# Small blocks' third layer as three split products, its weights through the ring of four stages

## What is computed

```python
h = gelu(x @ w1[e] + b1[e])        # 512 -> 1024, exact gelu
h = gelu(h @ w2[e] + b2[e])        # 1024 -> 1024
expert_out = h @ w3[e] + b3[e]     # 1024 -> 512
out = sum over the 2 best experts of gate * expert_out
```

## Time and profile before

| | us |
|---|---|
| median of 3 runs | 1721.82 |
| lowest, highest | 1720.84, 1722.42 |
| the profiled execution, its time | 1722.78 |
| its span in the trace | 1720.9 |

### The profile page before, as it was taken

One profiled execution on the slowest core, in us unless ns is written; L12 is line 12 of the kernel. 1 busy time (PEld: TensorE's weight loads), 2 busy tenths in 40 slices (PEclk: granted clock), 3 DMA queues, 4 the chain that ended last, 5 costly groups with the idle time before them and its releaser, 6 DMA issues.

```text
span 1720.9 us, 40335 instructions
## 1 busy us (share of the span) xinstructions
PE 1704.8 (99%) x15462; PEld 1509.2 (88%) x15462; DVE 1209.4 (70%) x2807; ACT 931.6 (54%) x1652; POOL 180.1 (10%) x271
## 2 busy tenths in 40 slices
PE   9999999999999999999999999999999999999997
PEld 8888888898889888988898878777899999999997
DVE  5677777777777777777775575566677777777773
ACT  4655656565556555655555454455545555545551
POOL 2010110111011101110110100000011010110100
PEclk9999999999999999999999999999999999999999
DMA  9982322222222222221215499998666666667662
GB/s 296 371 316 77 83 89 78 66 83 88 67 77 83 88 68 77 83 89 46 80 33 182 174 367 384 348 353 285 200 214 214 212 205 206 209 224 226 219 197 49
DMA packets 128181, 292.72 MB, mean 170 GB/s; under 512 B 19610, under 2 KB 42842, under 8 KB 128040
## 3 DMA queue, kind: packets, MB, share of 16 engines
q1 hardware_dynamic: 104616, 225.46, 38.8%
q0 software_dynamic: 23424, 65.30, 12.8%
HBM read 244.04 MB, written 46.66 MB: 169 GB/s over the span
## 4 chain that ended last, share of the span: by engine, by line
PE 88%; DVE 2%; issue 1%; ACT 1%; DMA 0%; POOLq 0%; POOL 0%; DVEq 0%; ACTq 0%
PE bank_rows L2301 21%; PE bank_rows L750 13%; PE bank_rows L736 12%; PE bank_rows L2316 7%; PE bank_rows L803 6%; PE bank_rows L2355 5%; PE bank_rows L791 4%; PE bank_rows L814 3%; PE bank_rows L2341 3%; PE bank_rows L2382 3%; PE bank_rows L830 2%; PE bank_rows L773 2%; PE bank_rows L894 2%; DVE probs L1470 1%; PE bank_rows L2393 1%
## 5 line engine op out<-in xcount | busy, mean ns | idle before, releaser
L1145 ACT ACTIVATE probs<-probs,neg_max 100x726 f32<-100x726 f32 x256 | 228.9, 896 | 168.1 <-DVE neg_max L1470 168.1
L2545 DVE TENSOR_TENSOR w_low<-stage,w_high 128x1024 fp32r<-128x1024 f32 x176 | 213.3, 1223 | 35.5 <-ACT w_high L2449 35.0
L1470 DVE CUSTOM_DVE_ANT_0 probs<-bank_rows,mask_sb 100x726 f32<-100x726 f32 x256 | 222.9, 909 | 16.4 <-PE bank_rows L791 14.8
L2449 ACT ACTIVATE w_high<-stage 128x1024 fp32r<-128x1024 f32 x176 | 183.9, 1057 | 33.4 <-DMA stage<-in_L_ffn_w 33.2
L2472 ACT ACTIVATE gelu<-bank_rows,biases 128x256 f32<-128x256 f32 x176 | 82.3, 474 | 216.4 <-PE bank_rows L2301 211.7
L1151 ACT ACTIVATE p_t<-bank_rows 122x1200 f32<-122x1200 f32 x128 | 146.4, 1168 | 95.8 <-PE bank_rows L803 95.8
L2301 PE MATMUL bank_rows<-h_high,w_high 128*128 128x256 f32 x704 | 196.5, 279 | 0.0
L2301 PE MATMUL bank_rows<-h_low,w_high 128*128 128x256 f32 x704 | 196.5, 279 | 0.0
L2301 PE MATMUL bank_rows<-h_high,w_low 128*128 128x256 f32 x704 | 196.5, 279 | 0.0
L736 PE MATMUL bank_rows<-ctx_high,wk_high 128*128 128x360 f32 (+1 forms) x512 | 175.7, 343 | 3.3 <-DVE v_even L1451 2.1
L736 PE MATMUL bank_rows<-ctx_low,wk_high 128*128 128x360 f32 (+1 forms) x512 | 167.8, 328 | 0.0
(11 more groups left out here) (245 smaller groups left out, 3869.9 us busy)
## 6 DMA issues: line engine op xcount, KB each, us to landing
stage<-in_L_ffn_w SPq DMA_DIRECT2D x240, 512.0 KB, 4.7
plain_w<-in_L_ffn_w SPq DMA_DIRECT2D x15, 2048.0 KB, 12.4
expert_in_rows<-filling POOLq DMA_DIRECT2D x8, 3341.0 KB, 25.2
router_rows<-in_gate_rows POOLq DMA_DIRECT2D x112, 200.0 KB, 3.4
ctx_raw<-in_ctx SPq DMA_DIRECT2D x16, 720.0 KB, 4.9
ctx_raw<-in_ctx SPq DMA_DIRECT2D x15, 724.0 KB, 4.3
xs_sb<-expert_in_rows SPq DMA_DIRECT2D x11, 514.0 KB, 5.4
b_sb<-in_L_ffn_b SPq DMA_DIRECT2D x19, 256.0 KB, 4.9
```

Of the source, the lines that this page charges most:

```text
L1145: nc.scalar.activation(p, p, ACT.Exp, bias=neg_max[:, h:h + 1], scale=-1.0, accum_out=exp_sum[:, h:h + 1]).then_inc(probs_ready, 1)
L1470: nc.vector.tensor_tensor_reduce(out=pieces(probs[:, q, :]), in0=slots_of(q)[0:S, :, 0:PIECE], in1=pieces(mask_sb[:]), scale=-1.0, scalar= ...
L2449: nc.scalar.activation(hi, src, ACT.Copy).then_inc(chunk_hi[which], 1)
L2545: nc.vector.tensor_tensor(lo, src, hi.bitcast(F32), ALU.subtract).then_inc(chunk_lo[which], 1)
```

## The change

w3 of the small blocks is no longer loaded plain. SP loads it in four pieces of two rows of tiles (load_third), through the same ring of stages, each after DVE has subtracted piece 4 + i of the same block's w2. ACT makes the high part (third_high), DVE the low one (third_low), into the buffers that the big blocks use for w3. The first four pieces of the next block's w2 wait for third_low where they waited for the subtractions of w2's pieces 4 to 7. The AHEAD pieces wait for third_low(7). The second gelu is done twice for each tile (once to fp32r, once whole), and DVE subtracts them by halves (second_split). The third layer has 24 split matmuls in place of 8 plain ones (16 in the trace). SP loads w2 pieces 0 to 3 before the w1 of the next but one block, as it did.

```diff
-    plain_loaded = {i: [sem(f"plain_w{i + 1}_loaded_{k}") for k in range(2)] for i in (0, 2)}
+    plain_loaded = [sem(f"plain_w1_loaded_{k}") for k in range(2)]
...
-    BASE = (0, HT * NSMALL, 0)
-    LOADS_BASE = HT * NSMALL // STAGES
+    BASE = (0, HT * NSMALL, HT // 2 * NSMALL)
+    SMALL_CHUNKS = HT + HT // 2
+    LOADS_BASE = SMALL_CHUNKS * NSMALL // STAGES
...
             else:
-                sp.wait_ge(chunk_lo[1], BASE[1] - STAGES + i + 1)
+                sp.wait_ge(chunk_lo[2], BASE[2] - STAGES + i + 1)
...
         def load_second(j, e, ks):
 
             for k in ks:
-                if HT * j + k >= STAGES:
+                if k >= STAGES:
                     sp.wait_ge(chunk_lo[1], HT * j + k - STAGES + 1)
+                elif j > 0:
+                    sp.wait_ge(chunk_lo[2], HT // 2 * (j - 1) + k + 1)
...
+        def load_third(j, e):
+            for i in range(HT // 2):
+                sp.wait_ge(chunk_lo[1], HT * j + HT - STAGES + i + 1)
+                rows = slice(2 * i * P, 2 * (i + 1) * P)
+                sp.dma_start(stage[:, i, :].rearrange("p (t n) -> p t n", t=2),
+                             as_rows(w3[bass.ds(e, 1), rows, :]).rearrange("(t p) n -> p t n", p=P)
+                             ).then_inc(chunk_loaded[i], 16)
...
         sp.wait_ge(early.first, HT // 2)
-        load_plain(1, e_next, 0)
+        load_plain(1, e_next)
         load_small_b3(0, e_now)
+        load_third(0, e_now)
         for j in range(NSMALL - 1):
             if j + 2 < NSMALL:
                 e_after = small_expert(j + 2)
-            if 0 < j < NSMALL - 2:
                 load_small_rows(j + 2)
             load_second(j + 1, e_next, FIRST_CHUNKS)
-            if j == 0:
-                load_plain(0, e_now, 2)
-                load_small_rows(2)
             if j + 2 < NSMALL:
                 sp.wait_ge(small_first, HT * (j + 1))
-                load_plain(j + 2, e_after, 0)
+                load_plain(j + 2, e_after)
             load_second(j + 1, e_next, LAST_CHUNKS)
-            if j == 0:
-                sp.wait_ge(early.y_ready, TPB)
-            else:
-                sp.wait_ge(y_ready, j)
-            load_plain(j + 1, e_next, 2)
             load_small_b3(j + 1, e_next)
             if j + 2 < NSMALL:
                 load_small_biases(j + 2, e_after)
+            load_third(j + 1, e_next)
             e_next = e_after
...
             for k in range(HT):
-                if k == 0:
-                    pe.wait_ge(plain_loaded[2][j % 2], 16 * (j // 2) + 16)
-                pe.wait_ge(small_second_gelu, HT * j + k + 1)
-                last = nc.tensor.matmul(small_y_bank(j)[:], small_h2[:, k, :], plain[2][j % 2][:, k, :],
-                                        start=(k == 0), stop=(k == HT - 1))
+                if k % 2 == 0:
+                    pe.wait_ge(chunk_lo[2], HT // 2 * j + k // 2 + 1)
+                if k % (HT // 2) == 0:
+                    pe.wait_ge(small_h2_lo, 2 * j + 2 * k // HT + 1)
+                for s, (a, c) in enumerate(PRODUCTS):
+                    last = nc.tensor.matmul(small_y_bank(j)[:], small_h2[a][:, k, :], w_hl[2][c][:, k, :],
+                                            start=(k == 0 and s == 0), stop=(k == HT - 1 and s == 2))
...
+        def third_high(j):
+            for i in range(HT // 2):
+                if j > 0 and i == 0:
+                    act.wait_ge(y_ready, j)
+                act.wait_ge(chunk_loaded[i], 16 * ((SMALL_CHUNKS * j + HT + i) // STAGES + 1))
+                nc.scalar.activation(w_hl[2][0][:, 2 * i:2 * i + 2, :], stage[:, i, :].rearrange("p (t n) -> p t n", t=2),
+                                     ACT.Copy).then_inc(chunk_hi[2], 1)
...
         for j in range(NSMALL - 1):
+            third_high(j)
             second_high(j + 1, FIRST_CHUNKS)
...
+        third_high(NSMALL - 1)
         for i in range(DT):
             chunk_high(0, i, ahead=True)
...
         for j in range(NSMALL - 1):
+            third_low(j)
             sums(j, 0)
...
                 split_first(j + 1, m)
+                if m % (HT // 2) == HT // 2 - 1:
+                    second_split(j, 2 * m // HT)
...
+        third_low(NSMALL - 1)
         for i in range(3):
             chunk_low(0, i, ahead=True)
```

More of the change, by code:

```diff
@@ L1949, in experts @@
     small_second_gelu = sem("small_second_gelu")
+    small_h2_lo = sem("small_h2_lo")
     y_ready = sem("ye_ready")
@@ L1969, in experts @@
             for i in range(3)]
-    plain = {i: [placed(f"plain_w{i + 1}_{a}", [P, *shapes[i]], F32, at[2 * i + a]) for a in range(2)] for i in (0, 2)}
+    plain = [placed(f"plain_w1_{a}", [P, *shapes[0]], F32, at[a]) for a in range(2)]
     h_hl = [[placed(f"h{i + 1}_{n}", [P, HT, BLOCK], F32R, h_at + H_SHIFT + (2 * i + a) * HT * BLOCK * 4)
@@ L1975, in experts @@
     small_h1 = [placed(f"small_h1_{n}", [P, HT, P], F32R, h_at + a * HT * P * 4) for a, n in enumerate(("high", "low"))]
-    small_h2 = placed("small_h2", [P, HT, P], F32, h_at + 2 * HT * P * 4)
+    small_h2_at = (h_at + 2 * HT * P * 4, start + SMALL_H_END + HT * BLOCK * 4)
+    small_h2 = [placed(f"small_h2_{n}", [P, HT, P], F32R, small_h2_at[a]) for a, n in enumerate(("high", "low"))]
+    small_h2_whole = placed("small_h2_whole", [P, HT, P], F32, small_h2_at[1])
     small_sums = placed("small_sums", [P, 2, D], F32, start + SMALL_H_END + 2 * HT * BLOCK * 4)
@@ L1994, in experts @@
     assert start + behind.at <= nc.sbuf_top
-    BASE = (0, HT * NSMALL, 0)
-    LOADS_BASE = HT * NSMALL // STAGES
+    BASE = (0, HT * NSMALL, HT // 2 * NSMALL)
+    SMALL_CHUNKS = HT + HT // 2
+    LOADS_BASE = SMALL_CHUNKS * NSMALL // STAGES
+    assert SMALL_CHUNKS % STAGES == 0 and HT // 2 == STAGES
     def place_in_ring(i, ahead):
@@ L2100, in load_small_biases, with load_plain @@
             load_biases(j, e, small_bias_loaded[j % 2])
-        def load_plain(j, e, which):
-            src = as_rows((w1, w2, w3)[which][bass.ds(e, 1), :, :]).rearrange("(t p) n -> p t n", p=P)
-            sp.dma_start(plain[which][j % 2][:], src).then_inc(plain_loaded[which][j % 2], 16)
+        def load_plain(j, e):
+            src = as_rows(w1[bass.ds(e, 1), :, :]).rearrange("(t p) n -> p t n", p=P)
+            sp.dma_start(plain[j % 2][:], src).then_inc(plain_loaded[j % 2], 16)
         def load_small_b3(j, e):
@@ L2114, in load_first @@
             src = as_rows(w1[bass.ds(e, 1), :, cols]).rearrange("(t p) n -> p t n", p=P)
-            sp.dma_start(plain[0][0][:, :, cols], src).then_inc(first_loaded[half], 16)
+            sp.dma_start(plain[0][:, :, cols], src).then_inc(first_loaded[half], 16)
         def load_second(j, e, ks):
             for k in ks:
-                if HT * j + k >= STAGES:
+                if k >= STAGES:
                     sp.wait_ge(chunk_lo[1], HT * j + k - STAGES + 1)
+                elif j > 0:
+                    sp.wait_ge(chunk_lo[2], HT // 2 * (j - 1) + k + 1)
                 sp.dma_start(stage[:, k % STAGES, :], as_rows(w2[bass.ds(e, 1), k * P:(k + 1) * P, :])
                              ).then_inc(chunk_loaded[k % STAGES], 16)
+        def load_third(j, e):
[5 more added lines that the diff above has]
+                             ).then_inc(chunk_loaded[i], 16)
         FIRST_CHUNKS, LAST_CHUNKS = range(0, STAGES), range(STAGES, HT)
@@ L2312, in output @@
                     if t == 0:
-                        pe.wait_ge(chunk_lo[2], CHUNKS_OF[2] * n + k // 2 + 1)
+                        pe.wait_ge(chunk_lo[2], BASE[2] + CHUNKS_OF[2] * n + k // 2 + 1)
                         pe.wait_ge(h2_lo, HT * n + k + 1)
@@ L2336, in first_layer @@
                 elif j > 0 and m == 0:
-                    pe.wait_ge(plain_loaded[0][j % 2], 16 * (j // 2) + (0 if j % 2 == 0 else 16))
+                    pe.wait_ge(plain_loaded[j % 2], 16 * (j // 2) + (0 if j % 2 == 0 else 16))
                 if HT * j + m >= 2:
@@ L2340, in first_layer @@
                 for k in range(DT):
-                    last = nc.tensor.matmul(first_bank[m % 2][:, 0:P], plain[0][j % 2][:, k, m * P:(m + 1) * P],
+                    last = nc.tensor.matmul(first_bank[m % 2][:, 0:P], plain[j % 2][:, k, m * P:(m + 1) * P],
                                             small_x[:, j % 2, k, :], start=(k == 0), stop=(k == DT - 1))
@@ L2502, in second_gelu @@
             act.wait_ge(small_turned, 2 * j + half + 1)
-            nc.scalar.activation(small_h2[:, m, :], turned_bank[half][:, i * P:(i + 1) * P], ACT.Gelu,
+            src = turned_bank[half][:, i * P:(i + 1) * P]
+            nc.scalar.activation(small_h2[0][:, m, :], src, ACT.Gelu, bias=bias_of(j, 1, m))
+            nc.scalar.activation(small_h2_whole[:, m, :], src, ACT.Gelu,
                                  bias=bias_of(j, 1, m)).then_inc(small_second_gelu, 1)
@@ L2634, in second_low, with third_low, second_split @@
                                         ALU.subtract).then_inc(chunk_lo[1], 1)
+        def third_low(j):
```

(12 more changed lines are left out.)

2 lines of the change are left out of this document (1 added, 1 removed).

## The result

The changed kernel takes 1744.09 us (1740.48 to 1749.22, four runs), the one before 1721.47 on the same chip: a ratio of 1.0132, 95% interval 1.0109 to 1.0155. It is slower, by 22.6 us where 9.1 were forecast, and lies just over the range's end of 1743. Its profiled execution is the longest of the four: 1749.22, span 1747.4. Against the span before (1720.9) that is +26.5.

What follows compares the result with a forecast made beforehand. PE bounds the kernel now, 26.26 us a small block; the change makes the buffer ring decide, at 26.85. Block 7 begins 3.0 later and its end costs 6.1: +9.1, profiled 1722.78 to 1731.9, median 1730.9; range 1717 to 1743.

Steps and rivals of the forecast that it cites:

- PE's saving: Third layer of small blocks: 24 split matmuls take 5.46 us instead of 6.87, saving 1.41 a block, 11.3 in all.
- ACT and DVE as no bound: Small blocks: added work brings ACT to 18.8 and DVE to 22.3 us, both below PE's 24.85.
- The ring decides: Small blocks: twelve pieces through four buffers make a cycle of 17.25 + L1 + L2, deciding once L1 + L2 exceeds 7.6.
- its fixed part: Ring cycle without landings: 13.6 from gelu to w3's last issue, 2.55 copy and subtraction, 1.1 to next gelu; 17.25 us.
- L1 + L2 = 9.6: Ring cycle's two landings, w3's last piece at 5.3 and w2's fourth at 4.3 us.
- L1: Time for w3's last piece to land in the ring cycle, taken as 5.3 us.
- L2: Time for the last of w2's first four pieces to land in the ring cycle, taken as 4.3 us.
- slower still: Rival: pieces meet scatter and w1, 5.8 and 5.2; cycle 28.25, +18, 1740 us; chance 0.17, a lower clock among it.
- PE's clock in the new waits: Rival: PE's clock falls in its new waits; at most 5.46 us more per third layer, a few giving 1740.
- The start: Block 0: w3's last piece lands 7.0 us after issue behind w1; first_gelu at 1020.5, where it was 1019.49.
- Block 7's begin: Last small block: begins at 1193.5 after six cycles of 26.85, where it was 1190.54; +3.0 us.
- The tail: End of block 7: waits for rows and small sums start its third layer 7.5 us late; +6.1 after its saving.

Runs made afterwards that it cites:

- own_stages_2: own_stages with block 0's w3 loaded before the next w2, one buffer elsewhere, sums(7, 1) before AHEAD's fifth subtraction: 1713.6, 0.9946 of the kernel before.
- own_stages: Changed kernel, but w3's pieces go to four buffers of their own and AHEAD pieces wait for w2's subtractions again: 1725.22, 0.9986 of the kernel before.
- late_scatter: Changed kernel, but POOL adds a block's rows to the output only after w2's first four pieces of block j + 2 are copied: 1749.79, ratio 1.0149.
- quarter_w1: Changed kernel, but from block 2 on only a quarter of each expert's w1 is loaded: 1745.6, 1.0134 of the kernel before.
- small_third: Changed kernel, but only a quarter of each w3 piece is loaded in small blocks: 1741.61, 1.0084 of the kernel before.
- warm_wait: Changed kernel with 16 unread matmuls on PE before its wait for the first gelu, blocks 1 to 7: 1753.38, 1.0149 of the kernel before.
- interleave: Changed kernel, but ACT and DVE take w2's first four pieces between the gelus of tiles 2 to 5: 1743.06, 1.0121 of the kernel before.
- late_gelu_10: Kernel before, with ACT repeating the first gelu ten times in blocks 1 to 7 so that PE waits: 1764.09, ratio 1.0247.
- late_gelu_6: Kernel before, with ACT repeating the first gelu six times in blocks 1 to 7 so that PE waits: 1744.82, ratio 1.0139.
- after_again: The changed kernel once more, unaltered, beside the first experiments: 1750.0, 1.0121 of the kernel before.

## Why the prediction was wrong in its size

*PE's saving* (1.41 a block): right. L2393 takes 5.51 where 5.46 was worked out, and own_stages_2 shows the PE-bound cycle of 24.84. *ACT and DVE as no bound*: right, by the same run.

*The ring decides*: right, and its fixed part too (14.0, 2.5 and 1.0 in the cycle above for 13.6, 2.55 and 1.1; the 0.4 is that cycle's longer gelu loop). That it is the sharing of buffers is shown by own_stages and own_stages_2, that it is neither the scatter nor w1's data by late_scatter and quarter_w1.

*L1 + L2 = 9.6*: the first term that failed. L1 was taken at 5.3, the median of a burst; but the chain runs through the *last* of the four pieces, and that took 5.9 in the mean, near the longest of the earlier trace rows (6.2, 6.1, 5.8) and not the median. L2 was taken at 4.3 from the spaced pieces of the big blocks (2.8 apart in the median), and was 5.3. Why is not shown: w3's last piece has landed before w2's fourth is issued (1099.55 and 1102.05), but w2's four are a burst of their own, 1.2 to 1.3 apart in that cycle, and with w3's bytes quartered (small_third) the fourth came later, not sooner. 11.2 in all, 1.6 more in each block. The forecast's "slower still" had 11.0 here, and its cycle of 28.25 is near the 28.46 of warm_wait, which kept the clock. That interleave has 28.25 too is chance: its loop is 9.30.

*PE's clock in the new waits*: the second, a term that the sum put at nothing. It stood as a rival with a bound for its price and no value. The profiled run shows what it does: 1.00 before the wait, 0.60 and 0.55 behind, a gelu loop of 7.7 in the mean for 6.64. That adds 1.1 to the cycle, 0.95 of it by the three loops with the lower level in them; the other 0.14 is DVE's, whose subtraction the third gelu waits for at a clock of 1.00 and which the forecast had put at no cost. 26.85 + 1.6 + 1.1 = 29.55, measured 29.41. The Trainium skill ("TensorE: Matmul & The Clock Gate", HAM oscillation) has a kernel whose clock falls back to half after each DMA wait between bursts of matmuls; by that, the traces agree in part: the clock fell in all seven blocks of late_gelu_10 (waits of 3.6) and in four of seven of late_gelu_6 (2.06), but not behind waits of 2.60 and 3.17 in the changed kernel. The Trainium skill's fit ("DMA: Bandwidth & Descriptors", Anatomy of one DMA) would have given 3.2 for 512 KB, an estimate for another path; the shortest piece of the changed kernel took 3.3, but the medians, 5.3 for w3's and 6.0 for w2's, are against it for a burst.

*The start*: 1020.14 for 1020.5. *Block 7's begin*: 1208.49 by the timeline, where it was 1189.97: +18.5 for +3.0. The six cycles are 2.56 longer than forecast, 6 x 2.56 = 15.4 of the 15.5. *The tail*: the third layer of block 7 ends 31.23 behind that begin (1239.72), before 23.49 (1213.46): +7.7 for +6.1. The rows were waited for 3.1 (2.9), small_sums 2.3 (some 5): together the waits are shorter than forecast, and the work between them is longer, since the clock was at its lower level in part of it. PE in the second half of second_layer(7), changed kernel; start to start is 0.43, and 0.23 once the clock is back:

```profile
1217.22 1.97 PE L2285 MATMUL bank_rows<-ident,xs_sb 128*128 128x128 f32 x8 [3.13 <-DMA xs_sb<-expert_in_rows]
...
1221.12 0.63 PE L2364 MATMUL bank_rows<-w_high,small_h_low 128*128 128x512 f32 x1
1221.55 0.63 PE L2364 MATMUL bank_rows<-w_high,small_h_high 128*128 128x512 f32 x1
...
1223.32 0.39 PE L2364 MATMUL bank_rows<-w_high,small_h_low 128*128 128x512 f32 x1
1223.55 0.40 PE L2364 MATMUL bank_rows<-w_high,small_h_high 128*128 128x512 f32 x1
```

In sum 15.5 and 1.6 over the forecast for the profiled run, which is the longest of the four: 1731.9 + 17.1 = 1749.0, measured 1749.22. The median run is 5.1 below the profiled one; it has no trace, but after_again shows how cycles of one program differ.

What stays open: why the last of four pieces takes 5 to 6 us on engines that were idle before. The runs exclude the scatter and w1 as the cause, and show that pieces of a quarter are there sooner (ACT takes the last 2.5 behind its issue, where it waits in part for PE), while w2's behind them then come later; whether it is the memory, the queue or the sixteen engines' descriptors was not tried.

## What to carry to other kernels

When work moves onto a shared ring of buffers, write down its cycle as a chain (last use, issue, landing, copy, free, and again for each turn) and compare it with the bound engine's block; the landing to put in is that of the last piece of the burst, not the median piece. If the ring is longer, buffers of its own for the new stream are worth more than a shift of order: here they turned 1.3% of loss into 0.1% of gain, and 0.5% with the ends put right, while the three shifts of order within the ring gained nothing that can be told. And price a new wait on PE above its length: in this kernel 1.3 us more in the mean at 2 us (0.3 where the clock stayed, 1.9 where it fell), 2.4 us more at 3.6 us.

## What the runs showed of the hardware that I had not expected

Waits of 2.02 us, alike to a few ns and between the same instructions, put the granted clock down in some blocks of late_gelu_6 and not in others, and a wait of 3.17 in the changed kernel left it at 1.00. Where it fell, PE was at half speed for several us (0.60 and 0.55 in two windows of 4 us of the changed kernel, behind a wait of 3.97). A kernel with 29 us less work for PE got no faster: its waits were longer, and its clock 0.50 in the two windows shown. And the DMA engines showed the same busy share, 0.96 to 1.02, at 349 and at 413 GB/s (the windows of the changed kernel), and 1.01 at 369 over 25 us in own_stages_2, where the kernel before had 0.99 at 350: a share near one did not mean that they were at their limit.
